# Two scattering edge passes of a graph network: gathers into rings of twelve steps, filled before the first scatter and then spread evenly

## What is computed

```python
h = relu(layernorm(x))                               # per node
deg = 1 + segment_sum(1, dst);  dinv = rsqrt(deg)
scaled = (h @ W + b) * dinv
x1 = x + (segment_sum(scaled[dst], src) + scaled) * dinv          # layer 0

h = relu(layernorm(x1));  up = h @ W_up
msg = segment_sum(m(up[src], edge_sh, mlp(edge_rbf)), dst)        # layer 1
A = msg @ W_lin;  B = polynomial(A)
o = B @ WB + h @ Wsc                                 # only nodes with an edge have B
out = x1 + normalize_over_nodes(o)                   # mean and variance over all nodes
```

## Time and profile before

| | before |
|---|---|
| median of three runs | 2046.6 us (2044.68 to 2050.34) |
| the profiled execution | 2046.1 us, span of its trace 2043.9 us |
| p1, E1, E2, E3, p2 (first to last instruction on the way) | about 141 to 710, 710 to 1057, 1058 to 1406, 1406 to 1645, 1645 to 2044 us |
| mean granted clock of PE | 0.962 |

### The profile page before, as it was taken

One profiled execution on the slowest core, in us unless ns is written; L12 is line 12 of the kernel. 1 busy time (PEld: TensorE's weight loads), 2 busy tenths in 40 slices (PEclk: granted clock), 3 DMA queues, 4 the chain that ended last, 5 costly groups with the idle time before them and its releaser, 6 DMA issues.

```text
span 2043.9 us, 53847 instructions
## 1 busy us (share of the span) xinstructions
PE 1728.9 (85%) x14740; PEld 1472.5 (72%) x14740; DVE 1710.5 (84%) x7602; ACT 1536.8 (75%) x3485; POOL 1191.1 (58%) x1166
## 2 busy tenths in 40 slices
PE   4988999999999889888857877775999967778885
PEld 3656888888888767777746666664888857777775
DVE  5777999999999878887838888885888879999885
ACT  3756878878787667877756667664999968889885
POOL 3103754455554567777756777776444229998751
PEclk9999999999999999999979899997999979999998
DMA  4669676666766567777745666667655549999994
GB/s 131 241 237 177 230 245 229 235 237 228 246 231 241 183 161 161 162 155 157 161 80 99 119 122 121 118 116 141 186 177 178 170 158 335 337 341 306 376 363 173
DMA packets 186260, 412.09 MB, mean 202 GB/s; under 512 B 48056, under 2 KB 73788, under 8 KB 186186
## 3 DMA queue, kind: packets, MB, share of 16 engines
q1 hardware_dynamic: 116634, 335.50, 47.3%
q0 software_dynamic: 56448, 74.95, 20.4%
q10 hardware_dynamic: 13104, 0.81, 1.6%
HBM read 207.34 MB, written 206.34 MB: 202 GB/s over the span
## 4 chain that ended last, share of the span: by engine, by line
PE 42%; DVE 13%; issue 12%; DMA 12%; POOL 10%; ACT 8%; SPq 1%; DVEq 1%; ACTq 0%; POOLq 0%
PE bank L842 16%; PE bank L822 5%; DVE st L1389 4%; DMA big<-in_x_dram,idx 4%; POOL big L529 4%; ACT hb L1126 3%; POOL msg_tab L540 3%; PE bank L983 3%; PE bank L801 3%; PE bank L838 3%; DMA big<-x_tab,idx 2%; DMA out_dram<-x1b 2%; PE bank L973 2%; POOL x_tab L540 2%; PE bank L862 2%
## 5 line engine op out<-in xcount | busy, mean ns | idle before, releaser
L1389 DVE BATCH_NORM_STATS2 st<-big 128x6 f32<-128x256 f32 x882 | 314.5, 412 | 82.3 <-DMA big<-x_tab,idx 64.1
L842 PE MATMUL bank<-o_rows,ht 128*128 128x256 f32 x1568 | 372.1, 379 | 0.0
L842 PEld LDWEIGHTS bank<-o_rows,ht 128*128 128x128 f32 x1568 | 298.7, 191 | 49.1
L822 PE MATMUL bank<-ident,hb 128*128 128x128 f32 x1568 | 210.8, 278 | 86.4 <-ACT hb L1126 69.6
L529 POOL DMA_INDIRECT big<-x_tab,idx x196 | 193.5, 987 | 149.4 <-issue 139.8
L495 POOL DMA_INDIRECT o_rows<-node_tab,idx x196 | 188.3, 961 | 137.9 <-issue 55.1
L822 PEld LDWEIGHTS bank<-ident,hb 128*128 128x128 f32 x1568 | 177.3, 142 | 116.4 <-issue 88.9
L1126 ACT ACTIVATE hb<-big,rs 128x256 f32<-128x256 f32 x392 | 216.4, 592 | 10.8 <-DVE rs L1412 10.1
L1087 ACT ACTIVATE hb<-big,rs 128x256 f32<-128x256 f32 x392 | 207.4, 590 | 21.2 <-DVE rs L1412 21.2
L1070 ACT ACTIVATE sd<-mv,eps_col 128x4 f32<-128x4 f32 (+1 forms) x343 | 101.0, 295 | 161.8 <-DVE mv L1398 160.4
L1025 PE MATMUL bank<-fin_w,ht 128*128 128x128 f32 x1568 | 203.3, 276 | 0.0
(11 more groups left out here) (267 smaller groups left out, 4486.7 us busy)
## 6 DMA issues: line engine op xcount, KB each, us to landing
big<-in_x_dram SPq DMA_DIRECT2D x97, 512.0 KB, 4.2
x_tab<-x1b SPq DMA_DIRECT2D x97, 512.0 KB
big<-x_tab SPq DMA_DIRECT2D x97, 512.0 KB, 5.8
out_dram<-x1b SPq DMA_DIRECT2D x97, 512.0 KB, 4.3
x_odd<-x1b SPq DMA_DIRECT2D x48, 512.0 KB
big<-x_odd SPq DMA_DIRECT2D x48, 512.0 KB
msg_tab<-zeros SPq DMA_DIRECT2D x50, 256.0 KB, 2.2
tpw_tab<-o_rows SPq DMA_DIRECT2D x49, 256.0 KB, 2.0
```

What stands on the lines that cost most here:

```text
L822: last = nc.tensor.transpose(bank[q][:, (2 * j + k) * P:(2 * j + k + 1) * P], hb[:, s.slot(2, 2), 2 * q + j, k * P:(k + 1) * P], ident[:])
L842: last = mm(y, ht[:, q, (2 * j + k) * P:(2 * j + k + 1) * P], w_sb[:, k, :], start=False, stop=(j == 1 and k == 1))
L1389: last = v.bn_stats(st[:, k, j, :], row)
```

## The change

The change has three parts. First, the lookups' pace: `pace` now counts groups; the 98 destination lookups go at four per group, the list steps at three operations per group as before, counted from group 24. Second, rings: `e1_rows` has twelve steps (four in `f_x`, eight in slots 4 to 7 of `big`), `e2_rows` twelve (eight in slots 0 to 3 of `big`, four in `f_x`). Twelve steps of E1 are gathered before E1's first scatter, the first four right behind the lookups and the others as p1 leaves the slots of `big`; ten steps of E2 before its first scatter. The rest is spread over the scatters by `rows_ahead`, at most one step's gather ahead of each scatter. Third, DVE and ACT run E1 and E2 in turns of twelve steps, because a ring's slot is fixed in the code (twelve steps ahead of the loop, three turns, then the rest). The first four gather steps of E3 move from behind E2's last gathers to ahead of its last four scatters, with fewer waits in front.

```diff
@@ tiles @@
+RING = 12
+        head_rows, tail_rows = (big[:, i:i + 4, :].rearrange("p b (h a d) -> p (b h) a d", h=2, a=2) for i in (0, 4))
+        e1_rows = [f_x[:, i] for i in range(4)] + [tail_rows[:, i] for i in range(8)]
+        e2_rows = [head_rows[:, i] for i in range(8)] + [f_x[:, i] for i in range(4)]
@@ POOL, lookups @@
-            def pace(n):
-
-                if n % 3 == 0 and n // 3 > 3:
-                    pool.wait_ge(p1["x1"].sem, 2 * (n // 3 - 3))
+            def pace(group):
+
+                if group > 3:
+                    pool.wait_ge(p1["x1"].sem, 2 * (group - 3))
             def dst_step(s):
-                pace(s.k)
+                if s.k % 4 == 0:
+                    pace(s.k // 4)
                 of_node_step(0, s.k)
             def list_step(s):
                 t = s.k
-                pace(T + 2 * t)
+                if t % 3 == 0:
+                    pace(T // 4 + 2 * t // 3)
                 landed(pool, list_out, s, 1)
...
-                pace(T + 2 * t + 1)
                 of_node_step(1, t)
@@ POOL, E1 and E2 @@
-            def gather(got_sems, s, which, table, free):
+            def gather(got_sems, s, which, table, free, rows):
...
+            def rows_ahead(k, first, last):
+
+                return [n for n in range(first, S) if (n - first) * (S - last) // (S - first) == k]
+
+            def e1_gather(k):
+                s = Step(0, k, k, S, 4)
+                gather(e1_got, s, 1, x, lambda s: done(pool, e1["relu"], s, RING), e1_rows[k % RING])
+
+            for k in range(4):
+                e1_gather(k)
+            for k in range(4, RING):
+                if k % 2 == 0:
+                    pool.wait_ge(p1["x1"].sem, 2 * (G - 4 + (k - 4) // 2))
+                e1_gather(k)
+
             def e1_step(s):
-                if s.live():
-                    gather(e1_got, s, 1, x, lambda s: done(pool, e1["relu"], s, 4))
-                if s.k == 4:
+                for k in rows_ahead(s.k, RING, 5):
+                    e1_gather(k)
+                if s.k == 0:
                     x1_landed(pool)
-                scatter_add(e1, e1_out, s, 4, x1_tab)
-
-            pool.wait_ge(p1["x1"].sem, 2 * (G - 4))
-            run_written_out(S, 4, e1_step)
+                scatter_add(e1, e1_out, s, 0, x1_tab)
+
+            run_written_out(S, 0, e1_step)
             all_landed(pool, e1_out, S, dmas=2)
+            def e2_gather(k):
+                s = Step(0, k, k, S, 4)
+                gather(e2_got, s, 2, x1_tab, lambda s: done(pool, e2["relu"], s, RING), e2_rows[k % RING])
+
+            for k in range(RING - 2):
+                e2_gather(k)
+            pool.wait_ge(pre["cleared"].sem, CLEARED)
             def e2_step(s):
-                if s.live():
-                    gather(e2_got, s, 2, x1_tab, lambda s: done(pool, e2["relu"], s, 4))
-                scatter_add(e2, e2_out, s, 5, msg_tab)
-                if s.k == S:
-                    pool.wait_ge(e3["relu"].sem, e3["relu"].base)
-                    all_landed(pool, e2_got, S, dmas=2)
+                for k in rows_ahead(s.k, RING - 2, 6):
+                    e2_gather(k)
+                if s.k == S - 5:
                     pool.wait_ge(pre["list_in"].sem, 16)
-                if s.k > S:
-                    k = s.k - S - 1
-                    gather(e3_got, Step(0, k, k, S, 4), 0, x1_tab, e3_free)
+                if s.k >= S - 4:
+                    k = s.k - (S - 4)
+                    gather(e3_got, Step(0, k, k, S, 4), 0, x1_tab, e3_free, xg[:, k])
+                scatter_add(e2, e2_out, s, 0, msg_tab)
-            pool.wait_ge(pre["cleared"].sem, CLEARED)
-            run_written_out(S, 5, e2_step)
+            run_written_out(S, 0, e2_step)
@@ ACT, E1 (and E2 alike) @@
-                        last = s_act(hg[:, a, i, :], xg[:, s.slot(1, 4), i, 0:D], ACT.Relu,
+                        last = s_act(hg[:, a, i, :], e1_rows[s.slot(1, RING)][:, i, 0:D], ACT.Relu,
-            run(act, S, 3, e1_step)
+            run(act, S, 3, e1_step, first=1, unroll=RING)
@@ DVE, E1 (and E2 alike) @@
-                    sums = edge_moments(e1, e1_got, s, 2)
+                    sums = edge_moments(e1, e1_got, s, 2, e1_rows[s.slot(0, RING)])
-            run(dve, S, 3, e1_step)
+            run(dve, S, 3, e1_step, first=1, unroll=RING)
```

More of the change, by code:

```diff
@@ L528, in gather @@
                     t = 2 * s.k + i
-                    pool.indirect_dma_start(xg[:, s.slot(0, 4), i, :], None, table, rows_of(idx3[:, which, t:t + 1])
+                    pool.indirect_dma_start(rows[:, i, :], None, table, rows_of(idx3[:, which, t:t + 1])
                                             ).then_inc(got_sems[s.slot(0, 4)].sem, 16)
@@ L571, in e3_free @@
                 landed(pool, ex_out, s, 4)
-            pool.wait_ge(pre["cleared"].sem, CLEARED)
-            run_written_out(S, 5, e2_step)
+            run_written_out(S, 0, e2_step)
             def e3_step(s):
                 if s.live() and s.k >= 4:
-                    gather(e3_got, s, 0, x1_tab, e3_free)
+                    gather(e3_got, s, 0, x1_tab, e3_free, xg[:, s.slot(0, 4)])
             run_written_out(S, 0, e3_step)
@@ L1188, in e2_step @@
                     for i in range(2):
-                        last = relu_row(h2[:, a, i, 1:ROW], xg[:, s.slot(1, 4), i, :], rs[:, 0, a], i)
+                        last = relu_row(h2[:, a, i, 1:ROW], e2_rows[s.slot(1, RING)][:, i, :], rs[:, 0, a], i)
                     last.then_inc(e2["relu"].sem, 1)
@@ L1213, in e2_step @@
                     merged_rows(e2, e2_out, s, 4, bank[7])
-            run(act, S, 4, e2_step)
+            run(act, S, 4, e2_step, first=1, unroll=RING)
             def e3_step(s):
@@ L1522, in scatter_to, with edge_moments @@
                 one.end()
-            def edge_moments(sm, got_sems, s, dmas):
+            def edge_moments(sm, got_sems, s, dmas, rows):
                 landed(dve, got_sems, s, 0, dmas=dmas)
-                return moments(sm, "chain_a", 0, [xg[:, s.slot(0, 4), i, 0:D] for i in range(2)], s)
+                return moments(sm, "chain_a", 0, [rows[:, i, 0:D] for i in range(2)], s)
             def take_own(sm, s, index):
@@ L1641, in e2_step @@
                     one.end()
-            run(dve, S, 3, e2_step)
+            run(dve, S, 3, e2_step, first=1, unroll=RING)
             dve.wait_ge(pre["list_in"].sem, 16)
@@ L1667, in e3_step @@
                 if s.live():
-                    sums = edge_moments(e3, e3_got, s, 2)
+                    sums = edge_moments(e3, e3_got, s, 2, xg[:, s.slot(0, 4)])
                 if s.live(1):
```

2 lines of the change are left out of this document (1 added, 1 removed).

## The result

The changed kernel takes 2066.7 us (median of three runs, 2064.8 to 2070.5) against 2046.6: the ratio is 1.010, 95% interval [1.007, 1.013]. The forecast was 2038, range 2028 to 2048. The time is near what the third rival gave (2063), but that is chance: the long turns are only one of the two causes, and the smaller one.

The account below looks back on a forecast made before the run. The prediction took the scatter's round trip to bound E1 and E2; 2.0 + 5.4 - 3.2 + 4.5 = 8.7 us gained from 2046.1 gave 2037.4, with the median's 0.5 2038 us, range 2028 to 2048.

Parts of the forecast that it names:

- the third rival: E1 and E2: turns of twelve stall DVE and ACT fetching code, 15 us per turn, giving 2063 us; chance 0.13.
- E2's body: E2's 48 scatter periods: 313.6 us against 318.1, 4.5 us gained.
- E1's body: E1's 48 scatter periods: 312.7 us against 318.1, 5.4 us gained as late gathered data goes.
- what bounds a step: E1 and E2: the scatter's round trip, 6.40 us without gathers; gathers inside it stick out by about 0.15 us.
- a gain of 20 us: Rival for E1 and E2: POOL's issue is the bound, all periods fall to 6.40, 20.7 us gained; chance 0.10.
- E2's head: E2 before its scatter 0: 22 gathers come first, so it starts at 1085.4 instead of 1082.18, 3.2 us lost.
- lookups and E1's head: Lookups end at about 678 instead of 707, p1 pays nothing, and E1's start gains 2.0 us.
- this cover: E1's head: p1 hides the early gathers; without that, scatter 0 stands behind 26 gathers, 9 us lost.
- the term of the sum: E1's head: DVE takes the odd group's load at 719.85 instead of 721.83, 2.0 us gained.
- the turns cost zero: DVE and ACT loops in E1 and E2: turns of twelve steps taken as costing nothing.
- the slack: E1 and E2: compute has 0.9 us spare per step, 10.8 per turn of twelve, to absorb a turn's cost.
- the four slots: E1's body: finished compute would next run into the four slots for rows to scatter; no size given.

Follow-up runs that it names:

- flat_late: Changed kernel with DVE's and ACT's E1 and E2 steps written out, no loop, and E2's index write at the end of DVE's step; 2045.0 us beside 2046.6.
- before_turns12: Kernel before with only DVE and ACT running E1 and E2 in turns of twelve steps; ratio 1.0075.
- before_turns8: Kernel before with only DVE and ACT running E1 and E2 in turns of eight steps; 2044.4 us beside 2046.6.
- after_flat: Changed kernel with DVE's and ACT's steps of E1 and E2 written out, no loop; ratio 1.0078.
- after_sidx_late: Changed kernel with E2's index write moved to the end of DVE's step; ratio 1.0028.

## Why the prediction was wrong, step by step

Two terms carried the forecast the wrong way. E2's body, put at 4.5 us gained, lost 15.1, 12 of it because a wait that the prediction had not followed up let an addition of DVE run into POOL's scatter, step after step. E1's body, put at 5.4 us gained, lost 6.9, 6 of it because the turns of twelve, put at nothing, stopped DVE. The gain in the bodies did not exist even without these two.

**Right: what bounds a step.** Gather-free scatters of the changed kernel lie 6.44 us apart at the least; POOL idles 3.0 us before them (1062.06 above). No kernel's median, with or without a gather, came under 6.4. Since the trace said so before, a gain of 20 us was ruled out rightly.

**Right: E2's head.** 27.5 us from first gather to scatter 0 forecast, 27.9 measured (1067.99 to 1095.92).

**Half right: lookups and E1's head.** They end earlier, the list phase starts at 303.1 (301 forecast), and p1 pays nothing. The list phase then took 398 us instead of 376, where I had kept its old length: its writes wait for each other's landing. In the kernels with the same pace the lookups ended anywhere from 672 to 703; 678 lies within. What sets this spread is open. I had priced the loss of this cover at 9 us against the kernel before; scatter 0 came 3.9 us later than before, and 8.6 us later than its data. But I put this neither into a rival nor into the range. With the cover, in flat_late, scatter 0 came at 727.6, 5.6 us earlier and not 2.0. The odd group's load was what came last, as I had said:

```profile
716.25 1.41 DVE L1418 BATCH_NORM_STATS2 st<-big 128x6 f32<-128x256 f32 x4 [2.27 <-DMA big<-x_odd]
```

This is 5.6 us before the 721.83 of the earlier trace rows. SP issued that load at 711.84 and not at 715.65, for the most part since p1's last x1 rows were done at 707.2 and not at 710.2. So some 2 of the 5.6 us are the term of the sum, and 3.8 are an earlier load. The change need not have brought those: p1 ends at 706.2 to 708.7 in all eleven other profiles, also at 707.7 and 708.4 in before_turns12 and before_turns8, whose lookups go as before. The profile that the forecast was worked out from has the latest end of p1.

**Wrong in size: the gain in the bodies (5.4 + 4.5).** I took the difference between the mean period, 6.628, and the quiet 6.553 to be gathers that land late all along, which rings would end. In flat_late, with rows twelve steps ahead and both faults gone, the median period with a gather is 6.56 in E1 and 6.58 in E2, against 6.58 and 6.57 before: nothing. The excess of before is mostly a few slow periods at the ends of a pass: the third from the start and the fourth from last of E1 (7.33 and 7.74) hold 2.0 of its 3.6 us, and the first four and the third from last of E2 (one of them 8.70) 3.5 of its 3.6. Such a period at E2's start, in the kernel before:

```profile
1088.99 1.62 POOL L540 DMA_INDIRECT msg_tab<-o_rows,sidx  x1 [0.30 <-issue]
...
1097.69 1.61 POOL L540 DMA_INDIRECT msg_tab<-o_rows,sidx  x1 [2.53 <-ACT o_rows L1132]
```

And one near E1's end in flat_late, with no gather left to be late:

```profile
1026.13 1.55 POOL L551 DMA_INDIRECT x_tab<-o_rows,sidx  x1 [2.95 <-DVE sidx L1550]
...
1033.72 1.55 POOL L551 DMA_INDIRECT x_tab<-o_rows,sidx  x1 [4.19 <-ACT o_rows L1161]
```

I read these as the filling and draining of the engines' pipelines. The rings leave them as they are: flat_late has 8.38 and 7.69 at E1's start, 7.44 and 7.59 at its end, and 8.43 at E2's start. The periods without a gather were put too low as well: 6.40 from three at E1's end, but 6.53 in the median of E1's twelve in flat_late.

**Wrong: the turns cost zero.** The step that failed is the slack: 0.9 us per step, "10.8 per turn of twelve". Slack adds up only while finished work may pile up, and here it may not: DVE is held by the four places of `sidx`, from 760 to 1020 us of the changed kernel in 27 steps,

```profile
DVE sidx L1544 <- DMA x_tab<-o_rows,sidx: 17.2, 27, 2.0
```

so the slack of each step is spent as a wait in that step. (In before_turns12 it is the ring of four gathered steps that holds DVE.) Of E1's two gaps, 5.4 and 4.5 us, 6 us are what the pass lost by its turns (6.772 against 6.648 per step in after_flat): some 2 us of each gap were absorbed, not 10.8. The rival's price, 15 us for a turn, was too high (2.6 to 5.4 here), its threshold of 10.8 too, and the four slots, which I had named for E1's body, were the reason. Its cause was present, and counting all of DVE's instructions, not the 336 that do work, would have given it more than 0.13.

**Not seen: E2's collision, 12 of the 25 us.** I asked what DVE would wait for next ("the four slots for rows to scatter") and didn't ask what that wait would align. A wait for the scatter's landing releases DVE and POOL in the same moment; the kernel before has no such wait in E2's quiet middle. The price could have been bounded: three stretched scatters stood in E2 of before, this one,

```profile
1084.10 1.79 POOL L540 DMA_INDIRECT msg_tab<-o_rows,sidx  x1 [0.30 <-issue]
```

0.2 us over the usual 1.57, another like it at 1099.61, and at 1379.94 one of 2.17, 0.55 over the usual 1.62. An estimate from these, 0.2 to 0.55 us in each of 48 steps, is 10 to 26 us. This would have been the rival that decides.

## What to carry to other kernels

Before prefetching deeper, take the periods one by one and see where the slow ones stand: here they stood at the ends of a pass, and no ring removed them. A faster producer will stop at the next bounded buffer; ask which event frees that buffer, who else starts on the same event, and whether these two hinder each other. Slack per step is no reserve for a long stall unless a queue is deep enough to hold it, and a loop body's length is to be counted in all its instructions.

## What the runs showed of the hardware

**A loop body that is too long costs 2.6 to 5.4 us of DVE for each way back** in the changed kernel and 3.1 to 3.5 in before_turns12: with 553 or 561 instructions in the body, and not with 370 or 376.

**An indirect DMA's issue on POOL is stretched by a DVE operation whose two inputs both lie in SBUF.** In E2 of the changed kernel, 40 of the 49 first scatters had the 0.55 us addition of L1660 running at their start. The 34 with the addition begun at most 0.21 us before took 1.83 to 1.98 us; the six with it begun 0.28 to 0.42 us before took 1.62 to 1.76; of the other nine, eight took 1.56 to 1.62. So it counts how much of the addition is left: begun 0.10 us before the scatter it costs 0.32 us, begun 0.30 us before (the scatter at 1125.07) 0.13. An addition of the same size with one input in PSUM costs nothing: 29 first scatters of after_sidx_late had L1625 running at their start and took 1.55 to 1.64. A gather went from 1.02 to 1.50 in after_flat. In E1 the median stays at 1.61 to 1.62 in all kernels. The Trainium skill ("SBUF — State Buffer", section "SBUF: two separate sides") says that a DVE operation with two SBUF inputs and a GpSimd operation that reads SBUF exclude each other, and that the one that comes second waits for the first to end. The trace agrees in one direction: DVE's operation keeps its 0.55 us, and POOL's, which begins 0.10 us into it, is 0.32 us longer. In the other it does not: in the kernel before, 45 additions of L1637 begin inside an issue of POOL and keep their 0.55 us too.
